# Feed-forward bias additions and operand sums on VectorE instead of GpSimd, from the third tile on

## What is computed

```python
x = x + xattn(layernorm(x), ctx_768, Wq, bq, Wk, bk, Wv, bv, Wo, bo)   # 16 heads, 64 keys
h = layernorm(x) @ W1 + b1                     # 512 -> 2048
q = h + (cos(th) * w_re + sin(th) * w_im) * w_im * sin(th + 0.1 * h) * 0.1
x = x + relu(q) @ W2 + b2                      # 2048 -> 512
```

## Time and profile before

| | |
|---|---|
| median of 3 runs | 2005.63 us (2000.49 to 2009.94) |
| the profiled execution's own time | 2007.17 us |
| its span, first to last instruction | 2005.4 us |
| mean granted TensorE clock | 0.995 of full speed |
| feed-forward part | from about 631 us on |

### The profile page before, as it was taken

How to read it: one execution, slowest core, us unless ns; L and a number is a source line. 1 busy time by engine, 2 the same in 40 slices (tenths; PEclk the granted TensorE clock), 3 DMA queues, 4 the chain that set the end, 5 groups by cost and what they waited for, 6 DMA issues and landing times.

```text
span 2005.4 us, 27939 instructions
## 1 busy us (share of the span) xinstructions
PE 1957.9 (98%) x9162; PEld 1625.9 (81%) x9162; DVE 1605.7 (80%) x2272; ACT 1261.5 (63%) x2132; POOL 749.9 (37%) x453
## 2 busy tenths in 40 slices
PE   9999999999999999999999999999999999999999
PEld 7788888888887788787887788788778878878877
DVE  8988888888876987888688778968878886886773
ACT  6767767666655876676477467546736755754661
POOL 6877777777774533202311320311131032031020
PEclk9999999999999999999999999999999999999999
DMA  7465664665536998787778688777877877876645
GB/s 245 149 164 140 171 170 129 174 177 152 157 100 209 315 338 269 263 247 235 263 242 251 223 265 258 244 261 235 237 259 244 253 240 253 257 235 228 225 138 189
DMA packets 347459, 441.29 MB, mean 220 GB/s; under 512 B 165552, under 2 KB 201392, under 8 KB 347312
## 3 DMA queue, kind: packets, MB, share of 16 engines
q1 hardware_dynamic: 346448, 439.44, 70.7%
q10 hardware_dynamic: 864, 0.04, 0.0%
HBM read 347.90 MB, written 91.23 MB: 219 GB/s over the span
## 4 chain that ended last, share of the span: by engine, by line
PE 56%; DVE 22%; ACT 11%; issue 9%; POOL 1%; DVEq 0%; DMA 0%; ACTq 0%; POOLq 0%
PE psum L1983 18%; PE psum L1985 17%; PE psum L1984 17%; DVE frac L1834 4%; ACT turns L1408 3%; DVE act_lo L1855 3%; DVE hid L1848 3%; PE psum L2076 2%; ACT frac L1384 2%; DVE acc L1867 2%; DVE stats L1517 2%; ACT x_sb L1208 2%; ACT act_hi L1436 1%; DVE late_hid L1848 1%; DVE late_hid L1805 1%
## 5 line engine op out<-in xcount | busy, mean ns | idle before, releaser
L1983 PE MATMUL psum<-w_ring,act_hi 128*128 128x512 f32 x1024 | 403.7, 394 | 27.2 <-DVE act_lo L1855 26.1
L1985 PE MATMUL psum<-w_ring,act_lo 128*128 128x512 f32 x1024 | 402.1, 393 | 0.0
L1984 PE MATMUL psum<-w_ring,act_hi 128*128 128x512 f32 x1024 | 402.0, 393 | 0.0
L1983 PE MATMUL psum<-xo,w_ring 128*128 128x512 f32 x784 | 307.6, 392 | 6.0 <-DVE late_hid L1822 3.6
L1985 PE MATMUL psum<-xo,w_ring 128*128 128x512 f32 x784 | 305.8, 390 | 0.0
L1984 PE MATMUL psum<-xo,w_ring 128*128 128x512 f32 x784 | 305.6, 390 | 0.0
L1834 DVE SCALAR_TENSOR_TENSOR frac<-frac,turns 128x512 f32<-128x512 f32 x256 | 223.5, 884 | 68.9 <-ACT frac L1384 68.0
L1983 PEld LDWEIGHTS psum<-w_ring,act_hi 128*128 128x128 f32 x1024 | 194.1, 190 | 73.9 <-issue 33.7
L1421 ACT ACTIVATE frac<-frac 128x512 f32<-128x512 f32 x256 | 156.4, 627 | 151.6 <-DVE frac L1834 151.6
L1985 PEld LDWEIGHTS psum<-w_ring,act_lo 128*128 128x128 f32 x1024 | 194.1, 190 | 40.8
L1984 PEld LDWEIGHTS psum<-w_ring,act_hi 128*128 128x128 f32 x1024 | 194.4, 190 | 40.0
(11 more groups left out here) (187 smaller groups left out, 4420.5 us busy)
## 6 DMA issues: line engine op xcount, KB each, us to landing
w_ring<-w2s SPq DMA_DIRECT2D x240, 512.0 KB, 4.1
w_ring<-w1s SPq DMA_DIRECT2D x392, 256.0 KB, 3.6
x_sb<-turn_dram SPq DMA_DIRECT2D x58, 512.0 KB, 6.0
res<-in_x SPq DMA_DIRECT2D x64, 256.0 KB, 3.6
x_dram<-res SPq DMA_DIRECT2D x64, 256.0 KB, 3.1
acc<-x_dram SPq DMA_DIRECT2D x16, 1024.0 KB, 8.1
x_sb<-in_x SPq DMA_DIRECT2D x15, 1024.0 KB, 6.3
x_sb<-x_dram SPq DMA_DIRECT2D x15, 1024.0 KB, 7.9
```

The lines of the kernel that those rows point to most:

```text
L1983: pe.matmul(o, a_hi, b_hi, start=first, stop=False, skip_group_check=resumed)
L1984: pe.matmul(o, a_hi, b_lo, start=False, stop=False, skip_group_check=resumed)
L1985: return pe.matmul(o, a_lo, b_hi, start=False, stop=last, skip_group_check=resumed)
```

## The change

The bias additions of tiles 2 to 15's rows, the bias additions of all 16 `acc` tiles and the operand sums of all seven pairs are done by VectorE, at fixed places of its order; GpSimd keeps the weight sums and the powers, without the waits on TensorE. The row loads of the following pair are issued at sweep accumulations 11 and 12 (the even tile's as soon as the low part of T4 is made), the load of the even `acc` tile at 7.

```diff
--- before.py
+++ after.py
@@ -73,6 +73,8 @@
 SWEPT = FC - 2
 XT_AT = (1, 2, 6, 8, 9, 10, 11)
 FIRST_XT_AT = (24, 25, 29, 30, 31)
+FIRST_SUMS_AT = (28, 29, 30, 31)
+T_SUMS_AT = (4, 5, 7, 8)
 SUMS_AT, SUMS_EACH = 2, 3
 GUARDED = TILES - 2
 CONSTS = 5
@@ -401,6 +403,9 @@
 
             T = i // KC + 2
             return 1 if i == 1 else T if i % KC == KC - 1 and T < TILES else None
+
+        def half_rows(part):
+            return slice(part * NB // 2, (part + 1) * NB // 2)
 
         def by_pair(row):
             return row.rearrange("p (g c) -> p g c", g=2)
@@ -752,7 +757,7 @@
                 elif T == PLAIN + 1:
                     sp.wait_ge(xt_lo_done, KC * (TILES + 2))
                 else:
-                    sp.wait_ge(xo_lo_done, NP * (T // 2 - 1))
+                    sp.wait_ge(xo_lo_done, NP * (T // 2 - 2) + (NP if T % 2 else OPERANDS.index("T4") + 1))
                 if T >= GUARDED:
                     sp.wait_ge(last_done, 1)
                     for blk in range(NB):
@@ -846,10 +851,10 @@
                                 rows_out(2 * T + 2 + s, half)
                         if at == second_half(T, 1):
                             store_acc(2 * T)
-                        if more and at == second_half(T, 3):
+                        if more and at == second_half(T, 7):
                             load_acc(2 * T + 2)
-                        if T + 2 < FFN_PAIRS and at == second_half(T, SWEPT - 1):
-                            for s in range(2):
+                        for s in range(2):
+                            if T + 2 < FFN_PAIRS and at == second_half(T, SWEPT - 3 + s):
                                 load_rows(2 * T + 4 + s)
             for blk in range(NB):
                 sp.wait_ge(y2_done, NB * (TILES - 1) + blk + 1)
@@ -903,15 +908,6 @@
                 rows = x_sb[T % 2][:, blocks, :]
                 pool.tensor_tensor(rows, rows, bo_row[:].unsqueeze(1).to_broadcast([P, NB // 2, C]), ALU.add)\
                     .then_inc(x1_whole, 1)
-
-            def add_last_bias(T, half):
...
             rsqrt(0)
 
@@ -1115,21 +1111,7 @@
                             t // TPB)
             pool.memset(ones[:], 1.0).then_inc(last_done, 1)
 
-            def operand_sums(T, names):
...
-            for j in range(FC + HALF1 + 4):
+            for j in range(FC + HALF1):
                 pool.wait_ge(turns_done, j + 1)
                 if j == 3:
                     rsqrt(TILES + 1)
@@ -1137,41 +1119,14 @@
                     pool.wait_ge(b2_in, 16)
                     pool.tensor_tensor(b2_row[:], b2_row[:], bo_row[:], ALU.add).then_inc(b2_biased, 1)
                     pool.wait_ge(b2_biased, 1)
-                if j in (4, 5):
-                    add_row_bias(2, j - 4)
                 if pair_summed(j) is not None:
                     add_parts(pool, pair_summed(j))
                 if j == 9:
                     rsqrt(TILES + 2)
-                if j in (11, 12):
-                    add_last_bias(0, j - 11)
-                if j in (FC + 1, FC + 2):
-                    add_row_bias(3, j - FC - 1)
                 if j == 20:
                     rsqrt(TILES + 3)
-            operand_sums(1, OPERAND_SUMS)
-            for half in range(2):
-                add_last_bias(1, half)
-            for T in range(1, FFN_PAIRS):
-                more = T + 1 < FFN_PAIRS
-                for p in range(FP):
-                    i = (T - 1) * FP + p
-                    if more and p < 2:
-                        for half in range(2):
-                            pool.wait_ge(prod, at_prod(i + (p if half else 0), "P7") - (NP - 2) * (p + half == 0))
-                            add_row_bias(2 * T + 2 + p, half)
-                    if more and p == 2:
-                        rsqrt(TILES + 2 * T + 2)
-                    if more and p == 4:
-                        rsqrt(TILES + 2 * T + 3)
-                    if p >= FP - 2:
-                        pool.wait_ge(prod, at_prod(i, "P7"))
-                        add_last_bias(2 * T, p - FP + 2)
-                if more:
-                    pool.wait_ge(y2_done, NB * (2 * T + 1))
-                    operand_sums(T + 1, OPERAND_SUMS)
-                for half in range(2):
-                    add_last_bias(2 * T + 1, half)
+            for T in range(4, TILES):
+                rsqrt(TILES + T)
 
             with pool.If_ne(count, P):
                 for s in range(2):
@@ -1866,6 +1821,32 @@
                     rows = acc[:, T % 2, n, :]
                     dve.tensor_tensor(rows, psum[:, Y2_BANK + n, :], rows, ALU.add).then_inc(y2_done, 1)
 
+            def add_row_bias(T, half):
+                dve.wait_ge(x_in[T % 2], x_loads(TILES + T))
+                rows = x_sb[T % 2][:, half_rows(half), :]
+                dve.tensor_tensor(rows, rows, bo_row[:].unsqueeze(1).to_broadcast([P, NB // 2, C]), ALU.add)\
+                    .then_inc(x1_whole, 1)
+
+            def add_last_bias(T, half):
+                dve.wait_ge(acc_in[T % 2], 16 * (T // 2 + 1))
+                if T == 0:
+                    dve.wait_ge(b2_biased, 1)
+                rows = acc[:, T % 2, half_rows(half), :]
+                dve.tensor_tensor(rows, rows, b2_row[:].unsqueeze(1).to_broadcast([P, NB // 2, C]), ALU.add)\
+                    .then_inc(acc_biased, 1)
+
+            def operand_sum(T, name):
+                j = OPERAND_SUMS.index(name)
+                if name == "T1":
+                    for half in range(2):
+                        dve.wait_ge(a_back[half], 16 * (turned_at(2 * T + 1) + 1))
+                else:
+                    dve.wait_ge(t_done, 4 * (T - 1) + j)
+                if name == "T4":
+                    dve.wait_ge(xo_lo_done, NP * (T - 1) + OPERANDS.index("B21") + 1)
+                a, b = {"T1": ("B12", "B11"), "T2": ("B22", "T1"), "T4": ("T2", "B21"), "T3": ("B22", "B12")}[name]
+                dve.tensor_tensor(PLACE[name], PLACE[a], PLACE[b], ALU.subtract).then_inc(t_done, 1)
+
             dve.wait_ge(par_sin, 1)
             dve.wait_ge(par_step, PAR_REDUCED + 4)
             dve.scalar_tensor_tensor(out=red[:, 0, :], in0=red[:, 6, :], scalar=1.0, in1=w_re, op0=ALU.mult,
@@ -1897,13 +1878,18 @@
                     layer_shift(TILES + 1)
                 if j in (5, 6):
                     turn_late_rows(1, j - 5)
+                if j in (6, 7):
+                    add_row_bias(2, j - 6)
                 if j in (7, 8):
                     layer_stats(TILES + 2, half_blocks(j - 7))
                 if j == 9:
                     layer_shift(TILES + 2)
                 if j in (11, 12):
                     turn_late_rows(2, j - 11)
+                if j in (13, 14):
+                    add_last_bias(0, j - 13)
                 if j in (18, 19):
+                    add_row_bias(3, j - 18)
                     layer_stats(TILES + 3, half_blocks(j - 18))
                 if j == 20:
                     layer_shift(TILES + 3)
@@ -1922,6 +1908,10 @@
                         sum_to_lo(pair_summed(j), half)
                 if j in FIRST_XT_AT:
                     operand_lo(1, FIRST_XT_AT.index(j))
+                if j in FIRST_SUMS_AT:
+                    operand_sum(1, OPERAND_SUMS[FIRST_SUMS_AT.index(j)])
+                if j in (30, 31):
+                    add_last_bias(1, j - 30)
             j = PLAIN * FC
             operand_lo(1, 5)
             wave(j - 1)
@@ -1948,6 +1938,9 @@
                     hidden_21(i)
                     hidden_22(i)
                     wave(chain_at(i, 0))
+                    if p == (0 if T > 1 else 2):
+                        for half in range(2):
+                            add_last_bias(2 * T, half)
                     if more and p in (1, 2):
                         layer_stats(TILES + 2 * T + 2, half_blocks(p - 1))
                     if more and p in (3, 4):
@@ -1959,6 +1952,13 @@
                     fraction(chain_at(i, 2))
                     positive_lo(first_half(T, 2 * p))
                     wave(chain_at(i, 1))
+                    if more and p == 0:
+                        for half in range(2):
+                            add_row_bias(2 * T + 2, half)
+                    if more and p in (2, 3):
+                        add_row_bias(2 * T + 3, p - 2)
+                    if p in (5, 7):
+                        add_last_bias(2 * T + 1, p // 6)
                 hidden_12(i)
                 positive_lo(first_half(T, FC - 1))
                 wave(chain_at(i, 2))
@@ -1972,6 +1972,8 @@
                         positive_lo(second_half(T, c + 2))
                     if more and c in XT_AT:
                         operand_lo(T + 1, XT_AT.index(c))
+                    if more and c in T_SUMS_AT:
+                        operand_sum(T + 1, OPERAND_SUMS[T_SUMS_AT.index(c)])
                 if not more:
                     add_outputs(2 * T + 1)
```

(7 more changed lines are left out.)

## The result

| | before | after |
|---|---|---|
| median | 2005.97 us (4 runs) | **1974.87 us** (1973.20 to 1976.68, 4 runs) |
| ratio | | 0.9847, 95% interval 0.9822 to 0.9872 |
| profiled execution, own time | 2007.17 us | 1976.68 us |
| mean granted clock, profiled | 0.995 | 0.998 |

31 us less, 1.5%; the forecast was 1975. First, from the page of the changed kernel, its span and part 1, with busy time, share and instructions of each engine, which answers to the earlier trace rows.

The account below looks back on a forecast made before the run. TensorE, 98% busy, was taken as the bound, waiting mostly for a VectorE stopped by GpSimd's large instructions. 3.3 - 0.8 + 3.2 + 17 + 2.4 = 25, plus 7 for the clock: 32 us off 2007.2, 1975 us, range 1965 to 1989.

Parts of the forecast that it names:

- The price of a half: One 128x1024 bias addition, half a tile's bias, on VectorE: taken as 1.15 us, against 2.4 to 2.8 on GpSimd.
- Steady pairs: Pairs 2 to 6 of the feed-forward part: 1.4 us of waits a pair in place of 5.0, 17 us in all.
- The lag limit: Steps 0 to 7 of a pair: VectorE's lag behind TensorE over 4.3 us costs TensorE time one for one.
- The floor: A pair without waits on TensorE: 720 matmuls at 0.2275 us, 163.8 us.
- First and last pair: First and last Strassen pair of tiles in the feed-forward part: fewer TensorE waits, gains of 3.2 and 2.4 us.
- Tiles 2 and 3: From 631 us, before the first pair: two waits go, 3.3 us gained; the wait for P1's copy grows by 0.8.
- Clock: Five half-rate stretches after waits of about 2 us cost 1.7 each; four taken as gone, 7 us.
- Rival A: VectorE's loop is fuller than reckoned, each added half costing 0.3 to 0.4 us more: 1988 us; chance 0.14.
- Rival B: Nothing is left to wait for: all 38 us of waits and the five half-rate stretches go, 1961 us; chance 0.06.
- C: Slower: VectorE's loop becomes the bound in steps 0 to 7, six pairs with 4.2 us more each, 2032; chance 0.04.
- D: GpSimd's instructions don't cause the long VectorE rows; moved work comes on top, partly hidden: 2000 to 2010 us; chance 0.04.
- SyncE's part: Row loads issued sooner and the acc load four accumulations later: they free nothing TensorE waits for, no gain.

Follow-up runs that it names:

- idle additions: The changed kernel, with GpSimd adding a tile nobody reads to itself at the old places, 12 times in each of six pairs and 4 in the last: 2008.42 us.
- loads back: The changed kernel with SyncE's row loads at accumulation 13 and acc's at 3, their old places: 1975.17 us.
- tile 1 later: The changed kernel with tile 1's two b2 halves moved from chunks 30 and 31 into step 0 of the first pair: 1975.89 us.
- sums only: The kernel before with only the operand sums moved to VectorE, GpSimd keeping all bias additions: 1994.50 us.

## Why the prediction was right, point by point

*What bounds the kernel.* Right, and shown: GpSimd's large additions stop VectorE, and VectorE's lateness reached TensorE. VectorE's stopped rows have no counterpart after; the idle additions bring them back, and the time.

*The price of a half.* 1.15 us taken, 1.14 in the timeline, 1.22 to 1.24 as duration. A repeated bias row and an in-place result cost nothing extra.

*Steady pairs.* Forecast 3.4 us each, 165.3 a pair; measured 168.8 to 165.4. The difference is right, its two parts are not, and that they cancel is luck. Against the true floor (next point) a pair lost 5.6 us before, not 5.0, and loses 2.2 after, not 1.4. The places fit less well still. By the distances of TensorE's starts the 2.2 are mostly 0.40 at P3 of step 1 (forecast 0.3, and 0.35 before the change already), 0.48 at P2 of step 5 (nothing forecast there), 0.3 in step 6 (0.65) and 0.8 in the first three accumulations behind step 7 (0.35), the largest part, which the list of waits shows only once (0.35, at the end of pair 6), since most of its gaps are too small for it. In step 5 TensorE waits for ScalarE's copy of P1, not at P3 for hidden_22; the larger entry for late_hid that was to show it fell instead, from 3.6 to 0.2 us. The lag limit itself was good: one more addition in step 4 costs all of its length.

*The floor.* 163.8 a pair was 0.6 too high. That didn't touch the forecast, which was a difference, but it made what was left look smaller than it was.

*First and last pair.* 3.2 and 2.4 us forecast. From its first P1 to the next pair's the first pair fell from 173.4 to 171.1, by 2.3; with 0.6 given back at the copy of P1 (below) its own part is 2.9. The last pair lost 4.45 us to waits and one half-rate stretch before, and nothing now: 2.7 without the stretch.

*Tiles 2 and 3.* This is the term that failed. "Where VectorE, 4 us less behind, has room" was wrong: behind the halves in chunks 6 and 7 stand two waits of 0.33 and 0.72 us (684.26 is the second), and 0.3 at the output sum remains. 3.3 us were forecast, 1.6 came. The copy of P1 waits 0.6 us longer (2.52 for 1.93) where 0.8 was forecast, and for the reason given.

*Clock.* Four of five stretches gone, 6.8 us, as taken. In the profiled executions this is a count: five in the kernel before, one after. It is partly luck: loads back and tile 1 later have the same wait for the copy of P1 or one nearly as long, and their profiled executions have no stretch behind it.

The sum as measured in the profiled executions: 1.6 - 0.6 + 2.9 + 17.0 + 2.7 + 6.8 = 30.4 of 30.5 us, where 32 were forecast. The forecast started from the profiled 2007.2, so by its own terms the changed kernel's profiled execution (1976.7) is the one to set against 1975; that the median of the four hits it within 0.2 us is chance. Rival A lost, though VectorE's loop is exactly as full as it feared; its extra 0.3 to 0.4 us for each half weren't there. Rival B's 1961 was out of reach for this placing, and was reached (1961.7) by another one. C and D are out by the pair period and by the idle additions. SyncE's part at nothing is shown by the loads put back.

## What to carry to other kernels

GpSimd is not a free helper beside a VectorE that reads two SBUF operands: count most of the length of each of its reading instructions on VectorE's chain (here 170 of 233 us), and look for VectorE rows three to four times as long as their undisturbed ones. Before moving work onto a fuller engine, don't ask for its share of the span but for the place in its order: the same 127 us of VectorE work in a pair cost TensorE 2.2 us or nothing. The floor is best taken from a whole stretch without a wait, not from twenty starts.

## What the runs showed of the hardware

- A GpSimd tensor_tensor that reads SBUF holds up a VectorE instruction of two SBUF operands: a 128x512 one ends 0.55 to 0.56 us after it, a 128x1024 one 1.08 to 1.09, in every such row of the kernel before and of the idle additions from 760 us on. VectorE rows with one operand in PSUM keep their 0.69 to 0.75 us beside it. GpSimd memsets of the same tile (0.95 us, and four in a row, 3.99) stop none.
- A GpSimd addition of 128x1024 took from 1.89 us up when both operands were the same tile, 2.4 and more with a repeated bias row.
- In all these traces, from 631 us to the last 20 us of a run, TensorE's clock fell to half rate only around waits of 1.85 us and more. Behind waits of about 2 us it stayed there for 3.4 us, and not behind each (5 of 15 in the kernel before). Twice it fell inside a longer wait at the first pair's P2 (4.67 us in sums only, 4.13 with the idle additions) and stayed for 6.8 us. The waits of 1.5 us and less in the later pairs of the idle additions have no stretch behind them.
- Over 13 executions of the kernel before, times go with the mean clock: 2002.1 us at 0.997, 2010.3 at 0.994. An estimate: 0.003 of 2005 us is 12 us at half rate, some 6 us lost, so most of the spread of 8 us between its runs is how many of these stretches an execution catches. The changed kernel's runs, at 0.998 to 1.000, spread by 3.5.
